# A sequence of four transformer layers' blocks on one core: the output projections' third share for ACT and POOL

## The chip, the cores and the metric

The kernel runs on one core of one Trainium2 chip. The metric is the device time of one execution in microseconds (us). The kernel before the change takes 793.25 us (median of 3 runs, 792.65 to 794.08).

The core has five engines with queues of their own: PE (TensorE, matrix products; PEld are its weight loads), DVE (VectorE), ACT (ScalarE), POOL (GpSimd) and SP (transfers). Each works through its own instructions in order; they meet through semaphores, which an instruction raises when it is done and on which a later one waits. Products land in PSUM, eight banks of 128 x 512 floats, which PE, DVE and ACT reach in this kernel; POOL works on SBUF alone.

## The reference

Two layers, each an attention and a feed-forward block with a residual and a layer normalisation behind each: attention with a position bias, a sparse Fourier product, dilated segment attention, and last a mixture of experts that is itself an attention. The change concerns only the end of the last block, for n = 2048 tokens (16 tiles of 128), 16 experts and 128 channels:

```
w = softmax(masked gates)                  # (n, 16), from the layer's input x
q, k, v = moe_proj(q_proj), moe_proj(k_proj), moe_proj(v_proj)
o = softmax(q k^T / sqrt(128)) v           # (n, 128)
out = einsum('ne,nh->enh', w, o) times o_proj, summed over e   # (n, 128)
x = layernorm(x + out)
```

So each tile of 128 tokens needs 16 products of its attention output with an expert's 128 x 128 matrix, each scaled per token by a gate weight w, and their sum, to which x is added before the normalisation.

## The kernel before

The kernel is one program with a written order for each engine; there is no planner. Up to about 718 us of the trace it computes the first three blocks and the last block's q, k, v and attention. Then come the output projections, the stage that the change rewrites.

The stage goes over 8 *pairs* of tiles; two pairs are a *quad* (4 tiles), and the final statistics are taken by quad. Variables: `a` is the pair's place in its quad, `u` the tile's place in its pair (0 or 1), `v` the quad's parity.

**PE.** Four experts side by side make a *group*, 128 x 512, one bank. Float products are split in two parts for accuracy, so a group is three matmuls (`product`, lines 1086 to 1088: high x high, high x low, low x high). The operand of a tile is its attention output in two parts: `op_hi` (a copy by ACT) and `op_lo` (the rest, a subtraction by POOL, `op_second`, line 591). A tile has four groups. The groups of experts 4 to 15 go to DVE (`group`, banks 0 to 3 in turn), the group of experts 0 to 3 goes to ACT (`first_group`, banks 4 to 7, two for each parity of pairs). In `out_quad` PE issues for each pair: DVE's groups of experts 4 to 7 of both tiles; the ACT groups of the *next* pair, which wait on `xc_set`, the op_lo of that pair; then DVE's other four groups.

**ACT.** `first_weighted` scales the four products of an ACT group by their weights, 128 columns at a time (line 1467), into `z_first` in SBUF, and raises `z0_sb` once a group. Then, once PE has done all DVE groups of the running pair, ACT copies the op_hi of the pair two further on; in each quad it also writes the normalised output of the quad before (`last_norm`, line 1490), which SP stores.

**POOL.** `first_sum` adds the four scaled parts of a tile: 256 columns onto 256 (line 657), 128 onto 128 (660), and the residual xb (662), into `y_acc`. In `sums_quad` POOL does, for each pair in order: the sums of tile 0 and tile 1 of the next pair; op_lo of both tiles of the pair after that (line 591); at the end of a quad the root of its variances (lines 678, 680).

**DVE.** Line 1891 multiplies each of the remaining products by its weight and adds it onto `y_acc`, 12 per tile, the two tiles in turn; the first of a tile waits for POOL's sum (`y0_set`). Each waits, through `acc_step`, until the last but one before it is done, which is the last one of the same tile. PE's bank waits go by the same `acc_step`. At a quad's end DVE takes the statistics (lines 1896 to 1906).

Of the kernel before, what the change touches and what calls it, by code (L numbers as in the profile page):

```python
# [23 lines left out]
ALU = mybir.AluOpType  # L24
ACT = mybir.ActivationFunctionType
# [34 lines left out]
E = 16  # L60
EPS = 1e-5
W3 = 3 * D
WC, NWC = 1024, 8
E_EARLY = NH // 2 * S // 4 // W3
LOADS_WE = 7
YR = 4


def build(nc, x, wq, wk, wv, wo, w_re, w_im, bias, w_qkv, w_out, sim, gates, p_q, p_k, p_v, p_o,
          ident, c_cos, c_sin, c_nsin, slopes, kpos, rank, rows, out):  # L70
    scale = float(DH) ** -0.5
# [5 lines left out]
    with ExitStack() as ctx:  # L77
# [44 lines left out]
        def bank(n, count=1):  # L122
            return psum[n // 4][:, n % 4 * QN:(n % 4 + count) * QN]
# [38 lines left out]
        w_cur = sb("w_cur", [P, QUAD, E])  # L162
        m_cur = sb("m_cur", [P, 2, 3])
        y_out = sb("y_out", [P, 2, QUAD, D])
        w_act = sb("w_act", [P, 2, 2, E])
        r_sum = sb("r_sum", [P, NT])
        kT_hi, kT_lo = sb("kT_hi", [P, NT * P], F32R), sb("kT_lo", [P, NT * P], F32R)
        f_p = probs[:].rearrange("p a b -> p (a b)")
# [70 lines left out]
        w_div, z0_ps, z0_sb, y0_set, w_act_set, y0_step = (  # L239
            sem(n) for n in ("w_div", "z0_ps", "z0_sb", "y0_set", "w_act_set", "y0_step"))  # L240
# [3 lines left out]
        v_set, acc_step, fin_step = sem("v_set"), sem("acc_step"), sem("fin_step")  # L244
        pool_step = sem("pool_step")
        q_hi_set, k_lo_set = sem("q_hi_set"), sem("k_lo_set")
        q_set, sc_ps, nmax_set, p_set, pt_ps, pt_sb, o_ps, o_sb = (
            sem(n) for n in ("q_set", "sc_ps", "nmax_set", "p_set", "pt_ps", "pt_sb", "o_ps", "o_sb"))
        fin_root = sem("fin_root")
        z_ps, w_set, fin_var, fin_std, fin_set = (  # L250
            sem(n) for n in ("z_ps", "w_set", "fin_var", "fin_std", "fin_set"))
# [222 lines left out]
        def _(pool):  # L474
# [165 lines left out]
            with pool.Fori(0, NT // 2 - 1) as i:  # L640
                for u in range(2):
                    t = 2 * i + u + 2
# [9 lines left out]
            def first_sum(pair, a, u, q, v):  # L652

                z, y = z_first[:, a, u], y_acc[:, v, 2 * a + u, :]
                n = 2 * pair + u
                pool.wait_ge(z0_sb, n + 5)
                pool.tensor_tensor(z[:, 0:2 * D], z[:, 0:2 * D], z[:, 2 * D:4 * D], ALU.add).then_inc(y0_step, 1)
                pool.wait_ge(y0_step, 2 * n + 1)
                pool.wait_ge(fin_set, q + 1)
                pool.tensor_tensor(y, z[:, 0:D], z[:, D:2 * D], ALU.add).then_inc(y0_step, 1)  # L660
                pool.wait_ge(y0_step, 2 * n + 2)
                pool.tensor_tensor(y, y, xb[:].rearrange("p t d -> p (t d)")[:, bass.ds(n * D, D)], ALU.add)\  # L662
                    .then_inc(y0_set, 1)

# [27 lines left out]
        def _(pe):  # L692
# [16 lines left out]
            for q in range(NQ):  # L709
# [4 lines left out]
                pair = bank(2 + 2 * (q % 2), 2)  # L714
# [169 lines left out]
            for n in range(-AHEAD, NU + 2):  # L884
# [8 lines left out]
                k = n - (NU - AHEAD)  # L893
# [189 lines left out]
            def product(dst, a, u, at, n):  # L1083

                hi, lo = op_hi[:, a, u, :], op_lo[:, a, u, :]
                pe.matmul(dst, hi, w_hi[:, at:at + n], start=True, stop=False)  # L1086
                pe.matmul(dst, hi, w_lo[:, at:at + n], start=False, stop=False)  # L1087
                return pe.matmul(dst, lo, w_hi[:, at:at + n], start=False, stop=True)  # L1088
# [70 lines left out]
            for b in range(NB):  # L1159
                with pe.Fori(b * KB // 2, (b + 1) * KB // 2 - b) as i:  # L1160
                    for u in range(2):
                        t = 2 * i + u
# [4 lines left out]

            def group(pair, a, n):  # L1170
                for u in range(2):

                    pe.wait_ge(acc_step, NT + 8 * (pair * 3 + n - 1))
                    product(bank((2 * (3 * a + n - 1) + u) % 4), a, u, E * W3 + n * 4 * D, 4 * D).then_inc(z_ps, 1)

            def first_group(pair, a):
                pe.wait_ge(xc_set, NT + QUAD + 2 * pair + 2)
                for u in range(2):
                    pe.wait_ge(z0_sb, 2 * pair + u + 1)
                    product(bank(4 + 2 * a + u), a, u, E * W3, 4 * D).then_inc(z0_ps, 1)  # L1180

            def out_quad(q, begin, end):
                for a in range(2):
                    pair = 2 * q + a
                    if not (begin and a == 0):
                        group(pair, a, 1)
                    if not (end and a == 1):
                        first_group(pair + 1, 1 - a)
                    group(pair, a, 2)
                    group(pair, a, 3)  # L1190


            pe.wait_ge(xc_set, NT + QUAD + 2)
            group(0, 0, 1)
            probs_T(NT - 1, 1)
            pe.wait_ge(pt_sb, 2 * NT + 2)
            first_group(0, 0)
            outputs(NT - 1, 1, NB - 1)
            pe.wait_ge(o_sb, NT + 2)
            out_quad(0, True, False)  # L1200
# [6 lines left out]
        def _(act):  # L1207
# [250 lines left out]

            def first_weighted(pair, a):

                act.wait_ge(z0_sb, 2 * pair + 4)
                weights_of(pair, a, NT // 2 + pair + 1)
                for u in range(2):
                    act.wait_ge(z0_ps, 2 * pair + u + 1)
                    act.wait_ge(y0_set, 2 * pair + u + 1)
                    for e in range(4):
                        ins = act.activation(z_first[:, a, u, e * D:(e + 1) * D],
                                             bank(4 + 2 * a + u)[:, e * D:(e + 1) * D], ACT.Copy,
                                             scale=w_act[:, a, u, e:e + 1])
                    ins.then_inc(z0_sb, 1)  # L1470

            def out_quad(q):
                for a in range(2):
                    pair = 2 * q + a
                    if pair + 1 == NT // 4:
                        act.wait_ge(w_div, 2)
                    if pair + 1 < NT // 2:
                        first_weighted(pair + 1, 1 - a)
                    if a == 0 and q:
                        last_norm(q - 1)  # L1480
                    act.wait_ge(z_ps, 6 * (pair + 1))
                    for u in range(2):
                        copy(op_hi[:, a, u, :], oT_all[:, bass.ds((2 * pair + 4 + u) % NT * P, P)])\
                            .then_inc(op_hi_set, 1)
# [19 lines left out]
        def _(dve):  # L1504
# [363 lines left out]
                dve.sem_inc(stored[u], 16)  # L1868


            per = QUAD * (E - 4)

            with dve.Fori(0, NQ // 2) as i:
                for v in range(2):
                    q = 2 * i + v
                    weights(q, NQ)
                    for a in range(2):
                        for n in range(1, E // 4):
                            for j in range(4):
                                for u in range(2):  # L1880
                                    t, e = 2 * a + u, 4 * n + j

                                    k = q * per + a * (per // 2) + 2 * (e - 4) + u
                                    z = bank((2 * (3 * a + n - 1) + u) % 4)[:, j * D:(j + 1) * D]
                                    if j == 0:
                                        dve.wait_ge(z_ps, q * 12 + a * 6 + 2 * (n - 1) + u + 1)
                                    if e == 4:
                                        dve.wait_ge(y0_set, q * QUAD + t + 5)
                                    else:
                                        dve.wait_ge(acc_step, NT + 8 + k - 1)  # L1890
                                    dve.scalar_tensor_tensor(out=y_acc[:, v, t, :], in0=z, scalar=w_cur[:, t, e:e + 1],  # L1891
                                                             in1=y_acc[:, v, t, :], op0=ALU.mult, op1=ALU.add)\
                                       .then_inc(acc_step, 1)
                    dve.wait_ge(acc_step, NT + 8 + (q + 1) * per)
                    for t in range(QUAD):
                        ins = dve.bn_stats(st[:, 0, t, :], y_acc[:, v, t, :])
                    ins.then_inc(fin_step, 1)
                    dve.wait_ge(fin_step, NT + 3 * q + 1)
                    dve.memset(tick[:, 0:1], 0.0).then_inc(fin_step, 1)
                    for t in range(QUAD):  # L1900
                        ins = dve.bn_aggr(mv[:, 0, t, :], st[:, 0, t, :])
                    ins.then_inc(fin_step, 1)
                    dve.wait_ge(fin_step, NT + 3 * q + 3)
                    dve.wait_ge(fin_std, q + 1)
                    dve.tensor_scalar(nb[:, 2 + v, :], mv[:, 0, :, 0], -1.0, None, ALU.mult).then_inc(fin_var, 1)
                    dve.tensor_scalar(ve[:, v, :], mv[:, 0, :, 1], EPS, None, ALU.add).then_inc(fin_var, 1)
# [48 lines left out]
```

## Time and profile before

| | |
|---|---|
| median of 3 runs | 793.25 us (792.65 to 794.08) |
| span of the profiled execution, first to last instruction | 791.8 us |
| its mean granted PE clock | 0.930 |
| busy: PE / DVE / ACT / POOL | 669.5 / 638.1 / 440.5 / 146.9 us |

The profile comes from one execution, whose time is given by its span; the runs' times hold what lies before and after it too. Busy time counts when an engine executes; idle time of an engine matters only where another waits for its result. [...] Matmuls overlap in PE's pipeline, so the distance between two starts, not the duration of one, says how fast they follow each other.

### The profile page before, as it was taken

What the parts mean: (1) busy time and instruction counts of PE and PEld (TensorE: products, weight loads), DVE (VectorE), ACT (ScalarE), POOL (GpSimd) and SP (SyncE); (2) the same over time, 40 slices, a digit from 0 to 9 for tenths busy, and PEclk for the clock granted to TensorE, in tenths of its full rate; (3) what the DMA queues carried; (4) which work ended last, traced back from release to release, by engine and by line L of the source; (5) the groups of instructions that cost most, each with busy time, mean ns of one, the idle gap of its engine ahead of it and who ended that gap; (6) DMA issues with size and microseconds to landing.
All of it is one profiled execution on the core that took longest, in us unless ns stands there. A gap on an engine that the chain in (4) does not pass through costs nothing.

```text
span 791.8 us, 16602 instructions
## 1 busy us (share of the span) xinstructions
PE 669.5 (85%) x5866; PEld 427.6 (54%) x5866; DVE 638.1 (81%) x1134; ACT 440.5 (56%) x961; POOL 146.9 (19%) x279
## 2 busy tenths in 40 slices
PE   7578888888888888899855886499999998998883
PEld 5223333333333333335634665499999997996652
DVE  2779999999999999965654667799999994554996
ACT  3059999999999999975442356111111114454442
POOL 6401000000000000001210117501111122123553
PEclk9569999999999999999975698599999999999998
DMA  7711111111111110006663000000000000000000
GB/s 201 223 25 33 33 32 33 31 33 31 33 32 32 32 31 3 2 3 137 134 171 95 4 5 1 0 1 1 0 1 0 0 0 1 0 0 1 14 14 26
DMA packets 28937, 28.72 MB, mean 36 GB/s; under 512 B 4952, under 2 KB 24920, under 8 KB 28152
## 3 DMA queue, kind: packets, MB, share of 16 engines
q1 hardware_dynamic: 27640, 26.99, 13.7%
q0 software_dynamic: 960, 0.79, 0.4%
q8 instruction: 41, 0.67, 0.4%
q14 instruction: 24, 0.20, 0.1%
q10 hardware_dynamic: 272, 0.07, 0.0%
HBM read 17.74 MB, written 4.98 MB: 29 GB/s over the span
## 4 chain that ended last, share of the span: by engine, by line
PE 52%; ACT 19%; issue 11%; DVE 10%; SPq 3%; DMA 2%; POOL 2%; ACTq 0%; DVEq 0%; POOLq 0%
ACT probs L1254 16%; PE ps_hi L775 13%; PE ps_lo L1086 7%; PE ps_lo L1088 7%; PE ps_lo L1087 7%; PE ps_hi L789 4%; PE ps_hi L1146 2%; DVE probs L1891 2%; PE ps_hi L1137 1%; DVE mx L1644 1%; PE ps_lo L975 1%; ACT mrow L1209 1%; PE ps_hi L819 1%; SPq L340 1%; PE ps_lo L1128 1%
## 5 line engine op out<-in xcount | busy, mean ns | idle before, releaser
L1561 DVE TENSOR_REDUCE mx<-ps_lo 128x2 f32<-128x1024 f32 x256 | 306.3, 1224 | 8.6 <-PE ps_lo L752 5.3
L1254 ACT ACTIVATE probs<-ps_hi 128x512 f32<-128x512 f32 x512 | 277.9, 597 | 44.0 <-PE ps_hi L775 31.0
L789 PE MATMUL ps_hi<-probs,v_blk 128*32 128x256 f32 x2048 | 164.7, 393 | 6.0 <-ACT mrow L1209 5.8
L775 PE MATMUL ps_hi<-q,k 28*128 28x512 f32 x512 | 129.7, 500 | 31.5 <-ACT probs L1254 14.6
L752 PE MATMUL ps_lo<-k,q 26*128 26x512 f32 x512 | 132.9, 516 | 4.6 <-DVE mx L1561 4.2
L1825 DVE SCALAR_TENSOR_TENSOR tok_cur<-ps_lo,w_cur,tok_cur 128x384 f32<-128x384 f32 x240 | 127.8, 609 | 6.1 <-PE ps_lo L1088 4.8
L775 PEld LDWEIGHTS ps_hi<-q,k 28*128 28x128 f32 x512 | 48.7, 183 | 141.5 <-ACT probs L1254 116.2
L1086 PE MATMUL ps_lo<-w_hi,op_hi 128*128 128x384 f32 (+1 forms) x304 | 108.1, 356 | 20.0 <-DVEq L1786 10.1
L1087 PE MATMUL ps_lo<-w_lo,op_hi 128*128 128x384 f32 (+1 forms) x304 | 105.5, 347 | 0.0
L1088 PE MATMUL ps_lo<-w_hi,op_lo 128*128 128x384 f32 (+1 forms) x304 | 105.5, 347 | 0.0
L789 PEld LDWEIGHTS ps_hi<-probs,v_blk 128*32 128x32 f32 x2048 | 42.0, 108 | 71.0 <-ACT probs L1254 59.2
L1209 ACT ACTIVATE op_hi<-xT 128x128 fp32r<-128x128 f32 (+1 forms) x40 | 10.0, 301 | 118.0 <-PE ps_lo L1088 118.0
L1086 PEld LDWEIGHTS ps_lo<-w_hi,op_hi 128*128 128x128 f32 x304 | 57.9, 191 | 28.2 <-DVE probs L1891 16.3
L555 POOL TENSOR_SCALAR mx_parts<-mx_all 128x8 fp32r<-128x8 f32 x32 | 7.4, 232 | 300.5 <-DVE mx_all L1555 293.6
L1088 PEld LDWEIGHTS ps_lo<-w_hi,op_lo 128*128 128x128 f32 x304 | 57.9, 191 | 2.1
L1087 PEld LDWEIGHTS ps_lo<-w_lo,op_hi 128*128 128x128 f32 x304 | 58.0, 191 | 1.3
L752 PEld LDWEIGHTS ps_lo<-k,q 26*128 26x128 f32 x512 | 49.4, 189 | 11.0 <-DVE mx L1561 9.4
L1891 DVE SCALAR_TENSOR_TENSOR probs<-ps_lo,w_cur,probs 128x128 f32<-128x128 f32 x192 | 50.5, 341 | 5.4 <-POOL probs L662 4.4
L591 POOL TENSOR_TENSOR op_lo<-xT,op_hi 128x128 fp32r<-128x128 f32 x40 | 17.9, 472 | 114.4 <-ACT op_hi L1209 114.4
L1146 PEld LDWEIGHTS ps_hi<-probs,v_tok 128*128 128x128 f32 x256 | 31.2, 193 | 2.4 <-DVE probs L1842 1.0
L1317 ACT ACTIVATE probs<-ps_lo 128x1024 f32<-128x1024 f32 x12 | 12.3, 1023 | 35.8 <-PE ps_lo L959 35.8
L1146 PE MATMUL ps_hi<-probs,v_tok 128*128 128x128 f32 x256 | 31.4, 276 | 0.8 <-DVE probs L1842 0.8
(256 smaller groups left out, 819.2 us busy)
## 6 DMA issues: line engine op xcount, KB each, us to landing
q<-q_parts SPq DMA_DIRECT2D x30, 192.0 KB
k<-k_parts SPq DMA_DIRECT2D x32, 96.0 KB
q_rep<-qk_p SPq DMA_DIRECT2D x24, 128.0 KB, 2.4
q_parts<-qk_hi SPq DMA_DIRECT2D x8, 256.0 KB, 4.8
k_rep<-qk_p SPq DMA_DIRECT2D x24, 64.0 KB, 2.1
xa<-in_L_attn_x SPq DMA_DIRECT2D x4, 256.0 KB, 3.3
q_parts<-qk_lo SPq DMA_DIRECT2D x4, 256.0 KB, 5.2
q<-mrow SPq DMA_DIRECT2D x64, 4.0 KB
```

Source lines behind the costliest of these rows:

```text
L752: mm = pe.matmul(bank(2 * (m % 2) + a), q0[rows, h * QN + i * P:h * QN + (i + 1) * P], k0[rows, k_at:k_at + QN], start=True, stop=True)
L775: mm = pe.matmul(bank(4 + (2 * n + a) % 3), k0[rows, k_at:k_at + P], q0[rows, h * QN:(h + 1) * QN], start=True, stop=True)
L789: mm = pe.matmul(o_bank()[32 * r:32 * r + 32, 0:OW], v_all[:, at:at + 32], probs0[:, n % P_RING, r * OW:(r + 1) * OW], start=(kb == 0), st ...
L1086: pe.matmul(dst, hi, w_hi[:, at:at + n], start=True, stop=False)
L1087: pe.matmul(dst, hi, w_lo[:, at:at + n], start=False, stop=False)
L1088: return pe.matmul(dst, lo, w_hi[:, at:at + n], start=False, stop=True)
L1146: mm = pe.matmul(bank(6 + u)[:, 0:P], v_tok[:, (b * KB + kb) * D:(b * KB + kb + 1) * D], pT_cur[:, u, kb * P:(kb + 1) * P], start=(kb == 0 ...
L1209: return act.activation(dst, src, ACT.Copy)
L1254: act.activation(probs0[:, n % P_RING, a * QN:(a + 1) * QN], bank(4 + (2 * n + a) % 3), ACT.Exp).then_inc(s0_free, 1)
L1561: dve.reduce_max(mx2[:, j % 2, :, i, kh], bank(2 * (m % 2), 2).rearrange("p (a n) -> p a n", a=2), AX_X).then_inc(max0_done, 1)
L1825: dve.scalar_tensor_tensor(out=tok_cur[:, a, u, :], in0=y, scalar=w, in1=tok_cur[:, a, u, :], op0=ALU.mult, op1=ALU.add).then_inc(y_free, 1)
L1891: dve.scalar_tensor_tensor(out=y_acc[:, v, t, :], in0=z, scalar=w_cur[:, t, e:e + 1], in1=y_acc[:, v, t, :], op0=ALU.mult, op1=ALU.add)\
```

## The change

For the second tile of each pair (u = 1) the group of experts 4 to 7 moves from DVE to ACT and POOL as well. Per pair ACT then scales three groups instead of two (`Z_FIRST`: tile 0's and tile 1's first group, and tile 1's second), POOL adds tile 1's second group onto its first, 512 columns wide, before it goes on as before, and DVE has 20 multiply-adds instead of 24, 12 for tile 0 and 8 for tile 1, in the order 0, 1, 0, 1, 0 four times (`Z_TURNS`). An instruction of DVE that follows one of the same tile waits for that one. DVE's five groups of a pair (`Z_LAST`) have the banks 0, 1, 2, 3, 7, ACT's three have 4, 5, 6, each one bank for every pair; a group waits until the same bank has been read in the pair before (`Z_READ`, the last reader's number). PE's order in a pair becomes: DVE's groups 0 and 1, the next pair's ACT groups 0 and 1, DVE's groups 2 and 3, the next pair's ACT group 2, DVE's group 4. `sums_quad` keeps its order.

```diff
+Z_FIRST = ((0, 0), (1, 0), (1, 1))
+Z_LAST = ((0, 1), (1, 2), (0, 2), (1, 3), (0, 3))
+N_FIRST, N_LAST = len(Z_FIRST), len(Z_LAST)
+Z_BANKS = (0, 1, 2, 3, 7)
+Z_TURNS = (0, 1, 0, 1, 0) * 4
+PER = len(Z_TURNS)
...
+Z_READ = [max(n for n, place in enumerate(Z_PLACES) if place[2] == d) for d in range(N_LAST)]
...
-                pool.wait_ge(z0_sb, n + 5)
+                pool.wait_ge(z0_sb, N_FIRST * pair + (5, 7)[u])
+                if u == 1:
+                    pool.tensor_tensor(z[:], z[:], z_first[:, a, 2], ALU.add).then_inc(y0_step, 1)
+                    pool.wait_ge(y0_step, 5 * pair + 3)
                 pool.tensor_tensor(z[:, 0:2 * D], z[:, 0:2 * D], z[:, 2 * D:4 * D], ALU.add).then_inc(y0_step, 1)
...
+            def group(pair, a, d):
+                u, n = Z_LAST[d]
+                pe.wait_ge(acc_step, NT + 8 + PER * pair - PER + Z_READ[d] + 1)
+                product(bank(Z_BANKS[d]), a, u, E * W3 + n * 4 * D, 4 * D).then_inc(z_ps, 1)
+
+            def first_group(pair, a, j):
+                u, n = Z_FIRST[j]
                 pe.wait_ge(xc_set, NT + QUAD + 2 * pair + 2)
+                pe.wait_ge(z0_sb, N_FIRST * pair + j + 2)
+                product(bank(4 + j), a, u, E * W3 + n * 4 * D, 4 * D).then_inc(z0_ps, 1)
...
                     if not (begin and a == 0):
+                        group(pair, a, 0)
                         group(pair, a, 1)
                     if not (end and a == 1):
-                        first_group(pair + 1, 1 - a)
+                        first_group(pair + 1, 1 - a, 0)
+                        first_group(pair + 1, 1 - a, 1)
                     group(pair, a, 2)
                     group(pair, a, 3)
+                    if not (end and a == 1):
+                        first_group(pair + 1, 1 - a, 2)
+                    group(pair, a, 4)
...
+            pe.wait_ge(o_sb, NT + 1)
+            for j in range(N_FIRST):
+                first_group(0, 0, j)
...
+                for j, (u, n) in enumerate(Z_FIRST):
+                    act.wait_ge(z0_ps, N_FIRST * pair + j + 1)
                     act.wait_ge(y0_set, 2 * pair + u + 1)
                     for e in range(4):
+                        ins = act.activation(z_first[:, a, j, e * D:(e + 1) * D],
+                                             bank(4 + j)[:, e * D:(e + 1) * D], ACT.Copy,
+                                             scale=w_act[:, a, u, 4 * n + e:4 * n + e + 1])
                     ins.then_inc(z0_sb, 1)
...
+                        for n, (u, e, d) in enumerate(Z_PLACES):
+                            t, k = 2 * a + u, (2 * q + a) * PER + n
+                            z = bank(Z_BANKS[d])[:, e % 4 * D:(e % 4 + 1) * D]
+                            if e % 4 == 0:
+                                dve.wait_ge(z_ps, (2 * q + a) * N_LAST + d + 1)
+                            if n < 2:
+                                dve.wait_ge(y0_set, q * QUAD + t + 5)
+                            else:
+                                dve.wait_ge(acc_step, NT + 8 + k - (Z_TURNS[n - 1] != u))
```

## Rows read from the trace of the kernel before

**Rows 1.** The page's busy tenths in 40 slices of 19.8 us: DVE and granted clock.
```profile
DVE  2779999999999999965654667799999994554996
...
PEclk9569999999999999999975698599999999999998
```

**Rows 2.** Windows: length; busy PE, PEld, DVE, ACT, POOL; clock; DMA, GB/s.
```profile
727.00:785.00 58.00, 44.82 (x175) 30.99 (x173) 55.68 (x231) 24.52 (x89) 33.67 (x66) 1.00 0.05 14
```

**Rows 3.** Lines of DVE from 725 to 785, by form: count, busy us, mean ns.
```profile
L1891 DVE SCALAR_TENSOR_TENSOR probs<-ps_lo,w_cur,probs 128x128 f32<-128x128 f32 x192 | 50.5, 341 | 5.4 <-POOL probs L662 4.4 <-DVE w_cur L1806 0.7 <-PE ps_lo L1088 0.2
```

**Rows 4.** Timeline of DVE in the stage: start, length, instructions merged.
```profile
727.62 12.50 DVE L1891 SCALAR_TENSOR_TENSOR probs<-ps_lo,w_cur,probs 128x128 f32<-128x128 f32 x47 [1.43 <-POOL probs L662]
740.15 0.87 DVE L1896 BATCH_NORM_STATS2 st<-probs 128x6 f32<-128x128 f32 x4
...
771.84 12.49 DVE L1891 SCALAR_TENSOR_TENSOR probs<-ps_lo,w_cur,probs 128x128 f32<-128x128 f32 x48 [0.22 <-DVE w_cur L1806]
```

**Rows 5.** Waits from 727 to 785: total us, times, longest.
```profile
PEld ps_lo L1086 <- DVE probs L1891: 16.3, 16, 2.3
```

**Rows 6.** Timeline of all engines, from one pair's ACT groups to the next's.
```profile
747.81 0.39 PE L1086 MATMUL ps_hi<-w_hi,op_hi 128*128 128x512 f32 x1
...
748.75 2.17 ACT L1467 ACTIVATE probs<-ps_hi,w_act 128x128 f32<-128x128 f32 x8 [2.16 <-issue]
...
749.20 0.39 PE L1086 MATMUL ps_lo<-w_hi,op_hi 128*128 128x512 f32 x1
...
749.97 0.74 POOL L657 TENSOR_TENSOR probs<-probs 128x256 f32<-128x256 f32 x1 [2.51 <-ACT probs L1467]
...
751.74 0.73 POOL L657 TENSOR_TENSOR probs<-probs 128x256 f32<-128x256 f32 x1
...
753.50 0.89 POOL L591 TENSOR_TENSOR op_lo<-xT,op_hi 128x128 fp32r<-128x128 f32 x2
...
754.52 0.49 PE L1086 MATMUL ps_hi<-w_hi,op_hi 128*128 128x512 f32 x1
```

**Rows 7.** Lines of POOL by form, whole span: count, busy us, mean ns.
```profile
L546 POOL TENSOR_TENSOR w_lo<-big,w_hi 128x1024 fp32r<-128x1024 f32 x8 | 19.1, 2420 | 19.7 <-ACT w_hi L1209 19.7
...
L657 POOL TENSOR_TENSOR probs<-probs 128x256 f32<-128x256 f32 x16 | 11.7, 733 | 24.6 <-ACT probs L1467 24.6
...
L678 POOL TENSOR_TENSOR rstd<-ve,half 128x4 f32<-128x4 f32 x4 | 4.1, 1018 | 9.1 <-DVE ve L1906 9.1
```

**Rows 8.** Timeline of all engines where the stage starts.
```profile
721.75 0.51 PE L1086 MATMUL ps_hi<-w_hi,op_hi 128*128 128x512 f32 x1 [0.78 <-DVE probs L1842]
...
722.79 2.17 ACT L1467 ACTIVATE probs<-ps_hi,w_act 128x128 f32<-128x128 f32 x8 [1.08 <-issue]
...
725.21 0.28 ACT L1209 ACTIVATE xT<-ps_hi 128x128 f32<-128x128 f32 x1 [0.24 <-PE ps_hi L1146]
...
725.54 0.50 PE L1086 MATMUL ps_hi<-w_hi,op_hi 128*128 128x512 f32 x1 [0.37 <-ACT xT L1209]
```

**Rows 9.** Timeline of PE: what follows an idle (its length in brackets).
```profile
397.72 0.50 PE L937 MATMUL ps_lo<-k_rep,q_rep 64*128 64x64 bf16 x6 [2.38 <-DVE mx L1644]
...
655.74 1.09 PE L1137 MATMUL ps_hi<-ident_sb,probs 128*128 128x128 f32 x8 [1.96 <-ACT probs L1209]
...
658.00 0.63 PE L1129 MATMUL ps_lo<-kT_lo,q_hi 128*128 x1
658.43 0.63 PE L1130 MATMUL ps_lo<-kT_hi,q_lo 128*128 x1
...
759.37 0.50 PE L1086 MATMUL ps_lo<-w_hi,op_hi 128*128 128x512 f32 x1 [1.85 <-DVE probs L1891]
```

**Rows 10.** Windows around two clock levels, columns as in rows 2.
```profile
397.60:400.60 3.00, 1.88 (x13) 1.48 (x13) 0.89 (x4) 2.84 (x9) 0.55 (x1) 0.50 0.46 114
...
657.00:660.00 3.00, 2.58 (x6) 2.11 (x7) 0.56 (x1) 0.47 (x1) 0.89 (x3) 0.50 0.00 0
660.50:663.50 3.00, 3.00 (x27) 2.91 (x26) 1.72 (x4) 0.59 (x2) 0.74 (x2) 1.00 0.02 5
```

More of the change, by code:

```diff
@@ L66, with z_places @@
 YR = 4
+Z_FIRST = ((0, 0), (1, 0), (1, 1))
[4 more added lines that the diff above has]
+PER = len(Z_TURNS)
+def z_places():
+    places, first, seen = [], [8 - 4 * (u == 0) for u in range(2)], [0, 0]
+    for u in Z_TURNS:
+        e = first[u] + seen[u]
+        seen[u] += 1
+        places.append((u, e, Z_LAST.index((u, e // 4))))
+    return places
+Z_PLACES = z_places()
+Z_READ = [max(n for n, place in enumerate(Z_PLACES) if place[2] == d) for d in range(N_LAST)]
 def build(nc, x, wq, wk, wv, wo, w_re, w_im, bias, w_qkv, w_out, sim, gates, p_q, p_k, p_v, p_o,
@@ L173, in build @@
         oT_all = xT
-        z_first = f_p[:, 0:2048].rearrange("p (a u n) -> p a u n", a=2, u=2)
-        y_acc = f_p[:, 2048:3072].rearrange("p (v t n) -> p v t n", v=2, t=QUAD)
+        z_first = f_p[:, 0:2 * N_FIRST * 4 * D].rearrange("p (a g n) -> p a g n", a=2, g=N_FIRST)
+        y_acc = f_p[:, 3072:4096].rearrange("p (v t n) -> p v t n", v=2, t=QUAD)
         ld_dft = sem("ld_dft")
@@ L655, in first_sum @@
                 n = 2 * pair + u
-                pool.wait_ge(z0_sb, n + 5)
+                pool.wait_ge(z0_sb, N_FIRST * pair + (5, 7)[u])
+                if u == 1:
+                    pool.tensor_tensor(z[:], z[:], z_first[:, a, 2], ALU.add).then_inc(y0_step, 1)
+                    pool.wait_ge(y0_step, 5 * pair + 3)
                 pool.tensor_tensor(z[:, 0:2 * D], z[:, 0:2 * D], z[:, 2 * D:4 * D], ALU.add).then_inc(y0_step, 1)
-                pool.wait_ge(y0_step, 2 * n + 1)
+                pool.wait_ge(y0_step, 5 * pair + (1, 4)[u])
                 pool.wait_ge(fin_set, q + 1)
                 pool.tensor_tensor(y, z[:, 0:D], z[:, D:2 * D], ALU.add).then_inc(y0_step, 1)
-                pool.wait_ge(y0_step, 2 * n + 2)
+                pool.wait_ge(y0_step, 5 * pair + (2, 5)[u])
                 pool.tensor_tensor(y, y, xb[:].rearrange("p t d -> p (t d)")[:, bass.ds(n * D, D)], ALU.add)\
@@ L1166, in _ @@
             outputs(NT - 2, 0, NB - 1)
[L1170 to L1176, printed above, removed]
+            def group(pair, a, d):
[4 more added lines that the diff above has]
+                u, n = Z_FIRST[j]
                 pe.wait_ge(xc_set, NT + QUAD + 2 * pair + 2)
-                for u in range(2):
-                    pe.wait_ge(z0_sb, 2 * pair + u + 1)
-                    product(bank(4 + 2 * a + u), a, u, E * W3, 4 * D).then_inc(z0_ps, 1)
+                pe.wait_ge(z0_sb, N_FIRST * pair + j + 2)
+                product(bank(4 + j), a, u, E * W3 + n * 4 * D, 4 * D).then_inc(z0_ps, 1)
             def out_quad(q, begin, end):
@@ L1185, in out_quad @@
                     if not (begin and a == 0):
+                        group(pair, a, 0)
                         group(pair, a, 1)
                     if not (end and a == 1):
-                        first_group(pair + 1, 1 - a)
+                        first_group(pair + 1, 1 - a, 0)
+                        first_group(pair + 1, 1 - a, 1)
                     group(pair, a, 2)
                     group(pair, a, 3)
+                    if not (end and a == 1):
+                        first_group(pair + 1, 1 - a, 2)
+                    group(pair, a, 4)
             pe.wait_ge(xc_set, NT + QUAD + 2)
+            group(0, 0, 0)
             group(0, 0, 1)
@@ L1196, in _ @@
             pe.wait_ge(pt_sb, 2 * NT + 2)
-            first_group(0, 0)
+            pe.wait_ge(o_sb, NT + 1)
+            for j in range(N_FIRST):
+                first_group(0, 0, j)
             outputs(NT - 1, 1, NB - 1)
@@ L1459, in first_weighted @@
             def first_weighted(pair, a):
-                act.wait_ge(z0_sb, 2 * pair + 4)
+                act.wait_ge(z0_sb, N_FIRST * pair + 1)
                 weights_of(pair, a, NT // 2 + pair + 1)
-                for u in range(2):
-                    act.wait_ge(z0_ps, 2 * pair + u + 1)
+                for j, (u, n) in enumerate(Z_FIRST):
+                    act.wait_ge(z0_ps, N_FIRST * pair + j + 1)
                     act.wait_ge(y0_set, 2 * pair + u + 1)
                     for e in range(4):
-                        ins = act.activation(z_first[:, a, u, e * D:(e + 1) * D],
-                                             bank(4 + 2 * a + u)[:, e * D:(e + 1) * D], ACT.Copy,
-                                             scale=w_act[:, a, u, e:e + 1])
+                        ins = act.activation(z_first[:, a, j, e * D:(e + 1) * D],
+                                             bank(4 + j)[:, e * D:(e + 1) * D], ACT.Copy,
+                                             scale=w_act[:, a, u, 4 * n + e:4 * n + e + 1])
                     ins.then_inc(z0_sb, 1)
@@ L1480, in out_quad @@
                         last_norm(q - 1)
-                    act.wait_ge(z_ps, 6 * (pair + 1))
+                    act.wait_ge(z_ps, N_LAST * (pair + 1))
                     for u in range(2):
@@ L1868, in _ @@
                 dve.sem_inc(stored[u], 16)
-            per = QUAD * (E - 4)
             with dve.Fori(0, NQ // 2) as i:
@@ L1877, in _ @@
                     for a in range(2):
[L1878 to L1894, printed above, removed]
+                        for n, (u, e, d) in enumerate(Z_PLACES):
[7 more added lines that the diff above has]
+                                dve.wait_ge(acc_step, NT + 8 + k - (Z_TURNS[n - 1] != u))
+                            dve.scalar_tensor_tensor(out=y_acc[:, v, t, :], in0=z, scalar=w_cur[:, t, e:e + 1],
+                                                     in1=y_acc[:, v, t, :], op0=ALU.mult, op1=ALU.add)\
+                               .then_inc(acc_step, 1)
+                    dve.wait_ge(acc_step, NT + 8 + (q + 1) * 2 * PER)
                     for t in range(QUAD):
```

## Prediction

> **What bounds the kernel now.** I read the page's slices first: the last three, from 732 us, are the output projections, which the change rewrites, and the DVE row shows 9, 9 and 6 there, the 6 holding the end [rows 1]. [...] By shapes nearly all of it is the multiply-adds of line 1891, 192 of them, 50.5 us, so 0.263 us from one start to the next though one lasts 0.341 [rows 3]. DVE's timeline shows them back to back in long runs, 47 in 12.50 us and 48 in 12.49 [rows 4]. Waits agree: the loads of PE's weights wait 16.3 us for DVE to free a bank [rows 5]. A pair of tiles costs DVE 24 x 0.263 = 6.3 us and half a quad's statistics, near 1 us: 7.3 us, and eight pairs fill the stage.
>
> Then I looked for what runs close behind. There is a loop from pair to pair through three engines, read from one stretch of the timeline [rows 6]. PE starts the two ACT groups of a pair at 747.81; ACT starts on the first at 748.75; POOL starts its sums at 749.97, needs 1.77 us for a tile (749.97 to 751.74) and 1.76 for the next, and only then, its queue being in order, makes the op_lo of the pair after (753.50, 0.89 us); PE starts that pair's ACT groups at 754.52. Round trip 6.71 us. It hides behind DVE's 7.3 by 0.6 us.
>
> **The change, part by part.** *DVE.* Eight pairs x 4 multiply-adds fewer: 32 x 0.263 = 8.4 us. The new order, tiles 0 1 0 1 0 repeated, puts tile 0 behind itself at three places inside a pair, and there the instruction waits for the one just before. The statistics behind the last multiply-add start 0.03 us after its end (740.12 to 740.15 [rows 4]), so such a step takes 0.34 + 0.03 = 0.37 instead of 0.26: 0.11 us, 24 times, 2.6 us. A lower bound is 0, the upper 0.3 each. DVE's own pair: 20 x 0.263 + 0.33 + 0.95 = 6.5 us. If nothing else were late, the stage would lose 5.8 us.
>
> *The loop.* The third ACT group (tile 1, experts 4 to 7) is only the fifth product that PE issues after op_lo: two ACT groups, two DVE groups, then it. POOL's sum of tile 1 waits for it, and op_lo of the next pair still stands behind that sum. The loop from op_lo to op_lo is now:
> - PE: two products took 1.39 us (747.81 to 749.20), so four take 2.78; from the fifth's start to ACT's start as now 0.94; and 0.10 more, since the first matmul after a wait lasts 0.49 instead of 0.39 (754.52 against 747.81) [rows 6]. 3.82.
> - ACT: four scalings and the hand-over to POOL, 748.75 to 749.97: 1.22.
> - POOL: the new 512-wide addition. The trace has none; 256 wide takes 0.733, 1024 wide 2.420 [rows 7]. On the line between them 512 takes 0.733 + (2.420 - 0.733)/3 = 1.30, which I take; the ends are those two rows. With 0.07 to the next instruction 1.37.
> - POOL: tile 1's sum as now, 1.77; op_lo 0.89 and 0.13 until PE starts: 1.02.
>
> Sum 9.20 us, against DVE's 6.5. DVE is no longer the bound; POOL's queue behind the third group is. Tile 0's sum costs the loop nothing: it fits between ACT's first and third group. So does the root at a quad's end, 1.02 us [rows 7]. Behind ACT's third scaling stand the final normalisation and the op_hi copies; they run beside POOL's 3.1 us of adding. PE's bank waits cost nothing: a DVE group waits until the same bank was read in the pair before, and DVE, which itself waits for tile 1's sum, is through by then; an ACT group, now with one bank instead of two, waits for a scaling that op_lo comes after anyway. At the start PE also waits for the last but one output's copy, done 2 us earlier. If DVE's lateness did reach a PE wait it would only lengthen the loop.
>
> [...]
>
> *The start.* The first three ACT groups instead of two, from 721.75, push the attention's last outputs 0.7 us back; ACT scales from 722.79, 2.17 us for two groups, so 3.3 for three, and its copy of the last output, at 725.21 today, comes near 726.1. PE starts pair 1's ACT groups at 726.4 instead of 725.54 [rows 8]. POOL, two of whose sums have the extra addition now, has summed pair 0 at 729.3 and pair 1 at 734.4; op_lo of pair 2 follows and its ACT groups start at 735.4.
>
> *The end.* Five more loops: pair 7's groups start at 735.4 + 5 x 9.2 = 781.4. Then 3.82 + 1.22 + 1.37 + 1.77 = 8.2: at 789.6 DVE takes up tile 1 of pair 7, with 19 multiply-adds left, 18 x 0.263 + 3 x 0.11 + 0.35 = 5.4, to 795.0. Today the last one ends at 771.84 + 12.49 = 784.33 [rows 4]. What follows (statistics, root, normalisation, store) is unchanged. **+10.7 us** with PE at the clock it has now.
>
> *The clock.* In the loop PE now has eight products, 5.6 us, and then nothing to do for 9.2 - 5.6 = 3.6 us, six times. Today its longest idle in the stage is 1.85 us, and the clock stays [rows 9]. [...] At 0.50 a 128x512 matmul comes 0.43 us after the one before (658.00, 658.43 [rows 9]) instead of 0.23 (1.39 for six [rows 6]), a product of three 1.29 instead of 0.69. [...] Bounds per loop: 0, and 5 x 0.60 = 3.0. A low stretch like the second, between 3 and 3.5 us at half speed, costs half its length if PE is busy in it, 1.6 us; I take this, six times: **+9.6 us**.
>
> Sum: span 791.8 + 10.7 + 9.6 = 812.1. The median of the runs, 793.25, lies 1.45 above the span, outside the first and last instruction, and that stays: 813.5.
>
> **The rivals.**
> 1. *The loop holds, the clock does too:* +10.7, so 804.0. For it: in this stage the clock never left 1.00, with 44.82 of 58 us of PE busy [rows 2]; the short bursts may be enough. [...]
> [...]
> 3. *Faster: DVE remains the bound.* Place: op_lo. Were it, or tile 1's sum, not in the way of PE, the stage would go at DVE's 6.5 us a pair, -5.8, so 787.5. It decides at 7.3 us a loop: below, the kernel is faster, above, slower. For it: POOL is busy for 33.67 of 58 us only [rows 2], and the loop hides today. Against it: it hides by 0.6, and four further products (2.8 us) and an addition of 1.37 enter it, while only tile 0's sum, 1.76, leaves it. Even with the addition at its lower end, 0.73, and no wait of PE, 8.6 remain.
> 4. *No change,* the loop near 7.3: 1.9 us of each round, the addition and more, would have to be hidden by something that I do not see; the time would stay at 793.3.
>
> **How the numbers follow.** Forecast 0.58 (813.5); rival 1 0.26 (804); rival 2 0.06 (822); rival 3 0.07 (787.5); rival 4 0.03 (793.3). The addition's ends change seven additions on the path by 7 x -0.57 = -4.0 and 7 x 1.12 = +7.8; the waits between neighbours on DVE at most 0.6, as only the last pair's count. The forecast's own range, with the clock costing 0.7 to 2.4 us a loop, is 806 to 819. Rival 1 with the addition at its lower end gives 800; part of rival 2 lies above 819. I give 800 to 820, which leaves out rivals 3 and 4, most of rival 2 and the edges of the rest, 2 in 10. About 0.2% is what a measurement of this kernel can tell from no change: faster 0.07, the same 0.03, slower 0.90.
>
> **What would show it.** Right: PE's ACT groups of one pair and the next 9 to 11 us apart; DVE waiting 2 us and more in each pair for POOL's last addition (the addition of xb), no longer PE for DVE; POOL's 512-wide addition near 1.3 us; multiply-adds 160 in number; granted clock 0.50 in stretches after idles of PE over 3 us. Wrong: PE's ACT groups less than 7.3 us apart, or op_lo ready before PE has done its DVE groups; a clock of 1.00 throughout would leave 804.

## The result: 814.6 us, 2.5% slower

The changed kernel takes 814.61 us (median of 4 runs, 813.5 to 817.22); the kernel before, beside it, 793.66 (4 runs, 792.65 to 795.42). The ratio is 1.0246, its 95% interval 1.0202 to 1.029. The profiled execution took 814.29 us with a span of 812.5, where the prediction had 812.1.

The slices of the page, DVE and granted clock (the share of its full speed that PE was given), answer to [rows 1]; a slice is 20.3 us now, and the stage fills the last four. There DVE reads 7, 6, 6, 5, where it had 9, 9, 6, and the clock 7, 8, 8, 7, where it had 9, 9, 8.

```profile
DVE  1789999999999999945545767899999965537665
PEclk9679999999999999999865996799999999997887
```

The stage from its first ACT group to its last multiply-add, as one window: length, then busy time (instructions) of PE, PEld, DVE, ACT and POOL, granted clock, DMA share, GB/s. First before, then after.

```profile
721.75:784.33 62.58, 49.70 (x202) 35.21 (x202) 55.73 (x230) 27.61 (x100) 36.42 (x70) 1.00 0.04 13
```

```profile
722.00:805.00 83.00, 57.36 (x202) 43.77 (x202) 51.65 (x198) 35.98 (x132) 46.81 (x78) 0.85 0.03 10
```

The stage is 20.4 us longer; the predicted sum was 20.3. DVE has 32 instructions fewer, as the change says, and ACT and POOL 32 and 8 more, but no engine is full any more, as DVE was before with 55.68 of 58.00 us [rows 2]: PE, the busiest now, works 57 of 83 us, at 0.85 of its full clock. Where nobody is full and everybody is late, a loop of waits is the first suspect. Two rows of the waits in this stage (total us, times, longest) name it:

```profile
PE ps_hi L1108 <- POOL op_lo L610: 19.3, 6, 3.4
DVE probs L1914 <- PE ps_lo L1110: 15.7, 6, 3.2
```

PE waits for POOL's op_lo, where its weight loads waited for DVE before [rows 5], and DVE waits for PE, whose products come behind the same wait. One turn of the loop in the timeline (start, length, instruction, in brackets the idle time before it and who ended it) answers to [rows 6]:

```profile
767.64 0.86 POOL L610 TENSOR_TENSOR op_lo<-xT,op_hi 128x128 fp32r<-128x128 f32 x2
...
768.63 0.49 PE L1108 MATMUL ps_hi<-w_hi,op_hi 128*128 128x512 f32 x1 [3.32 <-POOL op_lo L610]
...
769.83 2.37 ACT L1496 ACTIVATE probs<-ps_hi,w_act 128x128 f32<-128x128 f32 x8 [4.88 <-issue]
...
772.42 2.03 DVE L1914 SCALAR_TENSOR_TENSOR probs<-ps_lo,w_cur,probs 128x128 f32<-128x128 f32 x7 [2.00 <-PE ps_lo L1110]
...
773.96 1.14 ACT L1496 ACTIVATE probs<-ps_hi,w_act 128x128 f32<-128x128 f32 x4 [1.76 <-PE ps_hi L1110]
...
775.18 1.28 POOL L677 TENSOR_TENSOR probs<-probs 128x512 f32<-128x512 f32 x1 [2.33 <-ACT probs L1496]
...
778.29 0.87 POOL L610 TENSOR_TENSOR op_lo<-xT,op_hi 128x128 fp32r<-128x128 f32 x2
...
778.37 1.77 DVE L1914 SCALAR_TENSOR_TENSOR probs<-ps_lo,w_cur,probs 128x128 f32<-128x128 f32 x6 [1.61 <-POOL probs L684]
...
779.29 0.60 PE L1108 MATMUL ps_hi<-w_hi,op_hi 128*128 128x512 f32 x1 [3.33 <-POOL op_lo L610]
```

Read it downward: op_lo frees PE at 768.63; the third ACT group comes fifth, so ACT reaches it only at 773.96; POOL, which has waited 2.33 us, adds it at 775.18, then sums tile 1, and only then makes op_lo for the next pair, which PE gets at 779.29. That is 10.66 us a turn. The same turn cut by the granted clock:

```profile
769.50:772.60 3.10, 3.10 (x9) 2.38 (x8) 1.06 (x5) 2.29 (x8) 1.60 (x4) 0.50 0.00 0
773.00:776.00 3.00, 2.96 (x14) 2.10 (x12) 2.66 (x11) 2.04 (x7) 0.82 (x1) 1.00 0.00 0
776.00:779.20 3.20, 0.00 (x0) 0.00 (x0) 1.58 (x7) 1.14 (x5) 2.92 (x6) 1.00 0.27 82
```

PE has nothing to do from 776.00 on, as POOL works. In each of the six turns that begin behind such an idle the clock falls to 0.50, from 0.6 us before to 1.1 us after the first matmul of the burst (here 0.65 us after it, behind the idle of 3.32; 769.50 to 772.60 stands at 0.50), and is back at 1.00 before the burst ends. The chain of waits shows the last turn matmul by matmul (start, length):

```profile
789.00 0.86 POOL op_lo L610 x2
789.90 0.79 PE ps_hi L1108
790.69 0.43 PE ps_hi L1109
791.12 0.43 PE ps_hi L1110
...
792.83 0.43 PE ps_lo L1108
...
794.44 0.23 PE ps_hi L1108
...
795.44 0.89 ACT probs L1496 x3
796.39 1.29 POOL probs L677
...
799.80 0.09 issue
799.89 0.17 DVE probs L1914
```

Matmuls come 0.43 us apart until 793.25 and 0.23 after it: the low stretch lies on the five products that the loop waits for, here on the first three of them.

### The profile page after: what moved, and what is told of

The parts are those of the page before. It is cut to its first block and busy times, and to the rows that moved or that the text cites. A ratio compares the mean times of both kernels' runs of the same rounds, so it can differ in the third digit from the quotient of the medians.

```text
span 812.5 us, 16583 instructions
## 1 busy us (share of the span) xinstructions
PE 675.9 (83%) x5866; PEld 433.9 (53%) x5866; DVE 633.9 (78%) x1102; ACT 449.8 (55%) x993; POOL 157.6 (19%) x287
## 5 line engine op out<-in xcount | busy, mean ns | idle before, releaser
L1108 PE MATMUL ps_lo<-w_hi,op_hi 128*128 128x384 f32 (+1 forms) x288 | 102.0, 354 | 10.5 <-DVEq L1815 10.1
L1109 PE MATMUL ps_lo<-w_lo,op_hi 128*128 128x384 f32 (+1 forms) x288 | 100.2, 348 | 0.0
L1110 PE MATMUL ps_lo<-w_hi,op_lo 128*128 128x384 f32 (+1 forms) x288 | 100.0, 347 | 0.0
L1108 PEld LDWEIGHTS ps_lo<-w_hi,op_hi 128*128 128x128 f32 x288 | 56.0, 194 | 13.4 <-issue 10.1
L1914 DVE SCALAR_TENSOR_TENSOR probs<-ps_lo,w_cur,probs 128x128 f32<-128x128 f32 x128 | 37.6, 344 | 27.9 <-PE ps_lo L1110 15.7
L1109 PEld LDWEIGHTS ps_lo<-w_lo,op_hi 128*128 128x128 f32 x288 | 56.0, 194 | 1.6
L1110 PEld LDWEIGHTS ps_lo<-w_hi,op_lo 128*128 128x128 f32 x288 | 55.5, 193 | 1.8
L1496 ACT ACTIVATE probs<-ps_hi,w_act 128x128 f32<-128x128 f32 x96 | 27.0, 374 | 40.8 <-issue 29.0
L1108 PE MATMUL ps_hi<-w_hi,op_hi 128*128 128x512 f32 x32 | 15.9, 495 | 20.4 <-POOL op_lo L610 19.3
```

Of the source, the lines that this page charges most:

```text
L1496: ins = act.activation(z_first[:, a, j, e * D:(e + 1) * D], bank(4 + j)[:, e * D:(e + 1) * D], ACT.Copy, scale=w_act[:, a, u, 4 * n + e:4 ...
```

## The experiments

My theory had two parts: the new loop (PE's third group, ACT, POOL's addition, tile 1's sum, op_lo) is longer than DVE's share of a pair, about +10 us; and the idle that it leaves PE brings the low clock in nearly every turn, about +10 more. Rivals were other parts of the change that could cost by themselves: the bank layout of five and three, and DVE's neighbours of one tile. Each kernel is the changed kernel with the edit shown (the last one, experiment 6 with it). The stretch ahead of the stage, which no edit touches, starts the stage anywhere from 719.5 to 728.6 us in these profiled runs, so stages are compared as well as times.

**1. The third ACT group right behind the first two, on PE.** POOL's order is as changed, so op_lo still stands behind tile 1's sum, but the group is no longer fifth.

```
-  first_group(pair + 1, 1 - a, 0)
-  first_group(pair + 1, 1 - a, 1)
+  for j in range(N_FIRST):
+      first_group(pair + 1, 1 - a, j)
   group(pair, a, 2)
   group(pair, a, 3)
-  first_group(pair + 1, 1 - a, 2)
   group(pair, a, 4)
```

> The changed kernel with one thing moved: PE issues the next pair's third ACT group directly behind the first two, ahead of DVE's groups 2 and 3. Theory (the loop through the third group, ACT, POOL's sum of tile 1 and op_lo sets the stage): the third group is the third product after op_lo instead of the fifth, but ACT, which scales three groups in 3.21 us, is then in line: 0.94 + 0.10 until ACT starts, 3.21 + 0.12, the addition with its gap 1.36, the sum 1.77, op_lo and PE's start 1.0: 8.5 us a loop instead of 9.2 at full clock, PE's idle about 2.9 us instead of 3.4. Six to seven loops: 4 to 5 us less, near 810 (808 to 811), the clock still falling in most loops. Rival A (the bank layout, one bank for each of ACT's and DVE's groups, is what holds PE up): PE's order then changes nothing or makes it worse, 814 to 818. Rival B (DVE's order with neighbours of one tile): nothing, 814.6.

Measured: 803.62 us, ratio to before 1.0101 (1.0068 to 1.0135). The window of the stage, and ACT's scalings of two turns:

```profile
719.54:790.67 71.13, 53.47 (x202) 40.57 (x202) 49.80 (x198) 35.85 (x132) 46.90 (x78) 0.90 0.04 12
...
760.46 3.65 ACT L1494 ACTIVATE probs<-ps_hi,w_act 128x128 f32<-128x128 f32 x12 [4.45 <-issue]
...
769.37 3.20 ACT L1494 ACTIVATE probs<-ps_hi,w_act 128x128 f32<-128x128 f32 x12 [3.21 <-issue]
```

The place of the third group is worth 83.0 - 71.1 = 11.9 us of the stage. I had expected 4 to 5 us, a miss in size. The loop was sized well: between PE's first ACT groups of two pairs lie 8.43 and 8.36 us where the clock stays (8.5 expected). But I let the low clock cost as much as before. With the three groups in a row the loop goes through ACT's twelve scalings, 1.07 us a group, and PE at a clock of 0.50 needs 1.29 for one (three matmuls 0.43 apart), so a turn at the low clock is later by less: the scalings take 3.65 instead of 3.20 us, and the three turns with a low stretch take 8.80, 8.94 and 9.33 us, 0.4 to 1.0 more, where the changed kernel's lose 1.4 and more. The low clock itself became rarer too, 13.65 us in the stage instead of 25.5.

**2. op_lo ahead of tile 1's sum, on POOL.** PE's order is as changed.

```
-  for u in range(2):
-      first_sum(pair + 1, 1 - a, u, q + a, (v + a) % 2)
+  first_sum(pair + 1, 1 - a, 0, q + a, (v + a) % 2)
   for u in range(2):
       ...
       op_second((t + QUAD) % NT, a, u)
+  first_sum(pair + 1, 1 - a, 1, q + a, (v + a) % 2)
```

> The changed kernel with one thing moved: in POOL's queue op_lo of the pair after the next stands between the sums of tile 0 and tile 1 instead of behind both. Theory: the addition and the sum of tile 1, 3.1 us, leave the loop; it goes by PE's sixth product, ACT's third scaling and op_hi, op_lo: about 6.5 us, and 8.1 where ACT's final normalisation (1.65) stands ahead of op_hi, which is every second pair; 7.3 on average, as before the change. PE's idles shrink below 2.6 us, so the clock mostly stays at 1.00. Time 791 to 797. Rival A (bank layout) and rival B (DVE's neighbours): 814, unchanged. Rival C (POOL's whole load, 6.4 us of work a pair, is the bound, not its order): hardly less, 812 to 815.

Measured: 795.1 us, ratio 0.9985 (0.9954 to 1.0016), no difference from before. The window of the stage and PE's timeline:

```profile
723.67:786.40 62.73, 49.89 (x202) 36.30 (x202) 49.90 (x198) 35.62 (x132) 46.76 (x78) 0.96 0.05 14
...
746.50 0.50 PE L1109 MATMUL ps_lo<-w_hi,op_hi 128*128 128x512 f32 x1 [1.62 <-DVE probs L1915]
...
748.68 0.49 PE L1109 MATMUL ps_hi<-w_hi,op_hi 128*128 128x512 f32 x1 [0.45 <-POOL op_lo L610]
```

With op_lo out of tile 1's way the whole 20 us are gone: 62.73 against 62.58. PE waits for DVE again, 1.62 us here, and for op_lo only twice, 0.45 and 0.34. The low clock is down to 4.64 us of the stage though nothing was done about the clock: it went with PE's idle. (An idle of 2.05 us at 761.31 brought it, so the 2.6 us of the expectation was no safe mark.) The bank layout and DVE's neighbours are still here, so neither costs what was lost. Nothing is gained on the kernel before, though DVE has less to do: it waits 9.9 us in six times for POOL's sums, where it waited 4.4 in two.

**3. PE without the idle, the loop left as it is.** The second DVE group's product is made five times into the same bank (the last is the one that is read), so that PE works while POOL adds.

```
 def group(pair, a, d, again=0):
     ...
+    for _ in range(again):
+        product(bank(Z_BANKS[d]), a, u, E * W3 + n * 4 * D, 4 * D)
     product(...).then_inc(z_ps, 1)
...
-    group(pair, a, 1)
+    group(pair, a, 1, again=4)
```

> The changed kernel, and PE computes DVE's group 1 of each pair but the first five times over instead of once (the same product into the same bank; only the last one reports), 2.8 us of work put into the 3.4 us in which PE idles. Theory: the loop stays at 9.1 us, as PE has nothing to do there; the granted clock stays at 1.00 in the stage, and the time falls by what the clock cost, 1.6 to 1.8 us in each of six loops: 803 to 806, though PE does 84 matmuls more. If the low clock costs nothing (the loop then being longer for another reason): 814 or more. If the further products come in the way of DVE's group 1: up to 0.5 us a loop more than that, 807.

Measured: 804.29 us, ratio 1.0117 (1.0055 to 1.0179). The window of the stage and PE's ACT groups of two pairs:

```profile
720.01:792.98 72.97, 65.67 (x286) 51.85 (x286) 51.84 (x198) 35.40 (x132) 47.10 (x78) 1.00 0.04 11
...
760.87 0.49 PE L1108 MATMUL ps_hi<-w_hi,op_hi 128*128 128x512 f32 x1 [0.65 <-POOL op_lo L610]
...
769.97 0.49 PE L1108 MATMUL ps_hi<-w_hi,op_hi 128*128 128x512 f32 x1 [0.65 <-POOL op_lo L610]
```

84 matmuls that do nothing for the result make the stage 10.0 us shorter than the changed kernel's. The clock stays at 1.00 and a turn takes 9.10 us (predicted 9.20). So the loss splits: the loop costs 72.97 - 62.58 = 10.4, the clock 83.0 - 72.97 = 10.0. The split is good to some 0.4 us, for at the very end DVE now waits that long for the further products (POOL's last sum ends at 787.17, DVE goes on at 787.60).

**4. Half the filler.** The same with again=2.

> The changed kernel, and PE computes DVE's group 1 three times over instead of once: 1.4 us of work in the 3.4 us of idle, so that some 2.0 us remain in each loop. With the five-fold version the clock stayed at 1.00. Theory: an idle of 2.0 us among so much work brings fewer falls or none: at most 10 us of the stage at 0.50 (25.5 without the further products), the stage 73 to 77 us. If the falls come from the idle's place and not its length: 20 us or more at 0.50 and a stage of 80 or more.

Measured, one run: 816.84 us (its stage starts at 728.63). The window, and PE's ACT groups of three pairs, and two windows behind them:

```profile
728.63:807.55 78.92, 62.66 (x244) 48.50 (x244) 51.66 (x198) 35.75 (x132) 46.99 (x78) 0.91 0.04 11
...
761.96 0.50 PE L1108 MATMUL ps_hi<-w_hi,op_hi 128*128 128x512 f32 x1 [2.00 <-POOL op_lo L610]
772.64 0.49 PE L1108 MATMUL ps_hi<-w_hi,op_hi 128*128 128x512 f32 x1 [1.97 <-POOL op_lo L610]
781.73 0.49 PE L1108 MATMUL ps_hi<-w_hi,op_hi 128*128 128x512 f32 x1 [2.00 <-POOL op_lo L610]
...
762.10:765.10 3.00, 3.00 (x8) 2.37 (x9) 0.67 (x3) 1.61 (x6) 0.48 (x1) 0.53 0.00 0
772.80:775.80 3.00, 3.00 (x14) 2.46 (x15) 2.29 (x9) 2.12 (x8) 1.71 (x4) 1.00 0.00 0
```

A miss: I thought that half the filler would do more. Behind the idle of 2.00 us at 761.96 the clock was down (0.53 in the window from 762.10) and the turn took 10.68 us; behind the one of 1.97 at 772.64 it was at 1.00, and the turn took 9.09, the length of experiment 3. In all it was low for 14.5 us of the stage, and the idle's length alone does not say in which turn: idles of 2.02, 2.00, 2.00 and 1.92 us brought it, that of 1.97 did not.

**5. The addition made small.** again=2, and POOL adds 16 of the 512 columns; the rest of experts 4 to 7 of every second tile is left out of the sum.

```
-  pool.tensor_tensor(z[:], z[:], z_first[:, a, 2], ALU.add)
+  pool.tensor_tensor(z[:, 0:16], z[:, 0:16], z_first[:, a, 2, 0:16], ALU.add)
```

> The changed kernel, with two things: POOL adds only the first 16 of the third group's 512 columns (the rest of experts 4 to 7 of every second tile is left out of the result), and PE computes DVE's group 1 three times over instead of once, to keep its clock up. The loop of 9.1 us, with the clock at 1.00, loses what the addition costs above a small one, 1.29 - 0.2 = 1.1 us, seven times. Theory: the stage, from the first ACT group to DVE's last multiply-add, takes 72.97 us with PE kept busy and the whole addition; it takes 65 to 66 here, and ACT groups of neighbouring pairs stand 8.0 us apart. If the addition is hidden (rival: POOL's order matters, its length not): 73, and 9.1 us apart.

Measured: 796.49 us, ratio 1.0001 (0.9963 to 1.0039). The window, PE's ACT groups, and POOL's line by form (busy us, mean ns):

```profile
722.25:787.37 65.12, 55.84 (x244) 44.11 (x244) 50.78 (x198) 35.37 (x132) 38.65 (x78) 1.00 0.04 13
...
750.75 0.49 PE L1108 MATMUL ps_hi<-w_hi,op_hi 128*128 128x512 f32 x1 [0.94 <-POOL op_lo L610]
758.76 0.49 PE L1108 MATMUL ps_hi<-w_hi,op_hi 128*128 128x512 f32 x1 [0.93 <-POOL op_lo L610]
...
L677 POOL TENSOR_TENSOR probs<-probs 128x16 f32<-128x16 f32 x8 | 1.8, 222 | 6.4 <-ACT probs L1498 6.4
```

A turn takes 8.01 us, 1.09 less than the 9.10 of experiment 3, and the addition is 1.29 - 0.22 = 1.07 shorter: all of it stands on the loop. Even nearly free of it, the loop is longer than DVE's 7.3 us a pair before the change, from which on the change would have gained, so a faster addition alone does not save it.

**6. Both moves, and op_hi ahead of the normalisation.** Experiments 1 and 2 together; besides, ACT makes op_hi, which op_lo needs, before it normalises the quad that is done.

```
   # ACT, out_quad
-  if a == 0 and q:
-      last_norm(q - 1)
   act.wait_ge(z_ps, N_LAST * (pair + 1))
   for u in range(2):
       copy(op_hi...)
+  if a == 0 and q:
+      last_norm(q - 1)
```

> Both moves, and ACT copies op_hi before the final normalisation instead of after it. Theory: the loop is about 6.1 us in every pair (ACT's third scaling ends 4.4 after PE's start, op_hi 0.5, op_lo 0.9, hand-overs 0.3), under DVE's 6.5 a pair; DVE is the bound again and the stage gains what its 32 multiply-adds fewer give: 787 to 790, faster than before the change. POOL's 6.4 us a pair is close behind; if POOL is the bound instead, 789 to 792. Rivals A and B: 805 or more, since the layout and DVE's order are those of the change.

Measured: 797.39 us, ratio 1.0025 (0.999 to 1.006). The window, then DVE's and POOL's timeline:

```profile
728.60:790.01 61.41, 49.59 (x202) 36.52 (x202) 49.88 (x198) 35.73 (x132) 46.83 (x78) 0.97 0.05 14
...
756.09 3.71 DVE L1913 SCALAR_TENSOR_TENSOR probs<-ps_lo,w_cur,probs 128x128 f32<-128x128 f32 x13 [0.93 <-POOL probs L684]
...
763.16 1.02 POOL L701 TENSOR_TENSOR rstd<-ve,half 128x4 f32<-128x4 f32 x1 [1.28 <-DVE ve L1928]
```

A miss: I expected 787 to 790 us, and the stage is only 1.2 us shorter than before. DVE now waits for POOL's sums (0.93 us at 756.09), and POOL, whose queue is in order, waits 1.28 us at the quad's root for DVE's statistics, with the next sums behind it: each stands in the other's way.

**7. The root later too.** Experiment 6, and POOL takes the root of a quad behind op_lo of the next quad's first pair; POOL's loop over the quads is written out for this.

```
+  if a == 0 and q:
+      root_of(q - 1, 1 - v)
   first_sum(pair + 1, 1 - a, 1, q + a, (v + a) % 2)
```

> The version with both moves and op_hi first, and one thing more: POOL takes the root of a quad's variances behind op_lo of the next quad's first pair, instead of ahead of that quad's sums, where it waited about 1 us for DVE's statistics and kept the sums 1.3 us longer. Theory: in that version POOL's queue, full from pair 1 on, makes DVE wait 0.5 to 0.9 us in each second pair; without the root in the way DVE is the bound alone. The stage takes 59 to 60 us instead of 61.4 there and 62.6 before the change: 2.5 to 3.5 us faster than before, a ratio of 0.996. If POOL's whole load is the bound, 61 us, and a ratio of 0.998 to 1.0.

Measured: 794.88 us over 12 runs, ratio 0.996 (0.9926 to 0.9994) to the kernel before beside it (797.92). It is the one version here whose interval lies below 1, and only just: the kernel before moved by more between sets of runs (medians of 793.66, 795.04 and 797.92), so the gain rests on the stage of one profiled execution. The window, POOL's timeline at a root, and DVE's:

```profile
725.46:785.74 60.28, 49.33 (x202) 36.48 (x202) 49.89 (x198) 35.73 (x132) 46.81 (x78) 0.97 0.05 14
...
733.03 3.71 DVE L1914 SCALAR_TENSOR_TENSOR probs<-ps_lo,w_cur,probs 128x128 f32<-128x128 f32 x13 [3.12 <-POOL probs L684]
...
746.68 0.87 POOL L610 TENSOR_TENSOR op_lo<-xT,op_hi 128x128 fp32r<-128x128 f32 x2
747.51 1.01 POOL L704 TENSOR_TENSOR rstd<-ve,half 128x4 f32<-128x4 f32 x1
748.75 1.29 POOL L677 TENSOR_TENSOR probs<-probs 128x512 f32<-128x512 f32 x1
...
767.15 3.19 DVE L1914 SCALAR_TENSOR_TENSOR probs<-ps_lo,w_cur,probs 128x128 f32<-128x128 f32 x11 [0.81 <-POOL probs L684]
```

The root no longer waits. The stage is 2.3 us shorter than before. The relief itself is real: DVE has 55.73 - 49.89 = 5.84 us less to do. But it is idle for 60.28 - 49.89 = 10.4 us instead of 6.85, so 3.5 of the 5.84 turned into waits. For POOL's sums it waits 7.1 us in four times (0.81 at 767.15), where [rows 3] has 4.4. Of these 2.7 us more, 1.7 come once, at the stage's start: DVE's first run on both tiles waits 3.12 us at 733.03, where the kernel before has 1.43 [rows 4], since tile 1 of pair 0 now has the third group and its addition ahead of its sum. What would bring back the rest was not tried.

## Why the prediction held, and where it did not

*The loop.* Right in kind and size: 9.20 us a turn predicted, 9.10 measured where the clock is held; +10.7 predicted for the stage, +10.4 measured. Experiments 1 and 2 show that the order makes it: the one shortens the loop, the other breaks it, and they take back 11.9 and 20.3 us with the same work in the stage.

*The addition.* The line between the 256- and 1024-wide rows [rows 7] gave 1.30 us; it measures 1.286. In proportion to the 1024-wide row alone it would have been 1.21; the 0.222 us that 16 columns take (experiment 5) shows a part of the time, about 0.19 us, that does not shrink with the width.

```profile
L677 POOL TENSOR_TENSOR probs<-probs 128x512 f32<-128x512 f32 x8 | 10.3, 1286 | 13.6 <-ACT probs L1496 13.6
```

*The clock.* The weakest step beforehand was my estimate of 1.6 us a loop, from one low stretch (657 to 660 at 0.50, 1.00 again from 660.5 [rows 10]) and from the idles of 1.96 and 2.38 us about which the clock stood at 0.50 [rows 9, rows 10], both shorter than the 3.6 us to come. It came out: 9.6 predicted, 10.0 measured. The idles are 2.64, 3.35, 3.34, 3.32, 3.33 and 3.28 us (3.6 predicted), and each brought a fall. That the sum fits so well is in part luck: the prediction had six falls alike. Five of them last 3.4 us, and cost 1.4 to 1.6 us where two neighbouring turns show it (a turn less 9.10), and one, from 745.4, lasts 6.8 us and costs 2.8. The rest of the 25.5 us, 1.6 us, lies behind PE's last product. Rival 1, the same loop with a full clock, was put at 804.0; experiment 3 is that kernel, and takes 804.29. Rival 2 (822) had the clock at 0.50 through the whole stage; it was there for 25.5 of 83.0 us.

*The steps of the ACT groups.* Predicted 10.8 us apart (9.2 + 1.6), measured 9.00, 10.53, 11.94, 10.66, 10.66 and 10.61; the five from 735.50 to 789.90 make 10.88 on average, and 735.50 itself was put at 735.4.

*DVE's waits: half wrong.* I wrote that DVE would wait for POOL's last addition and "no longer PE for DVE". The second holds but for 0.9 us; the first does not, as a bound of each pair: three pairs have it, 1.6 us each, and 3.0 and 3.1 us lie at the stage's start. In the lines of DVE, by form (count, busy us, mean ns, idle before and by whom):

```profile
L1914 DVE SCALAR_TENSOR_TENSOR probs<-ps_lo,w_cur,probs 128x128 f32<-128x128 f32 x128 | 37.6, 344 | 27.9 <-PE ps_lo L1110 15.7 <-POOL probs L684 11.0 <-DVE w_cur L1835 0.7
L1914 DVE SCALAR_TENSOR_TENSOR probs<-ps_hi,w_cur,probs 128x128 f32<-128x128 f32 x32 | 11.1, 346 | 2.3 <-PE ps_hi L1110 1.9
```

DVE waits longer for PE (15.7 us) than for POOL's sums (11.0). Three of the five DVE groups of a pair come behind the next pair's ACT groups in PE's queue and so behind its op_lo; the prediction had DVE through with a pair by then. It did not show in the time, as the loop took what was predicted without it.

*DVE's own share.* 160 multiply-adds (128 and 32 in these rows), as the count said. Their price was right too: 8.4 - 2.6 = 5.8 us less, and 5.84 in experiment 7.

*Rival 3, DVE as the bound.* Rightly given little, but its price was wrong. I put the stage at 5.8 us less once op_lo was out of the way; experiments 2, 6 and 7 take it out of the way and get nothing, 1.2 and 2.3 us. The step that failed there is that DVE would then be full: POOL with 46.8 us of work in 60 and an order to keep is late with its sums, for which DVE waits 9.9, 8.4 and 7.1 us in these three, 1.7 of the surplus over 4.4 at the stage's start alone.

## What to carry to other kernels

Before moving work from a full engine to an idle one, follow the loop that comes back to its start, in order of each queue: here 5.8 us less on the bound put four products and an addition into a loop with 0.6 us to spare, and took only one sum out of it. Then look at what the new idle does to TensorE's clock; here that was half of the loss, 10.0 of 20.4 us. And when such a move fails, change the order before giving it up: here one sum moved behind op_lo took back all 20 us.

## What the hardware showed that I had not expected

- Nearly the same idle brought the low clock in one turn and not in another: in experiment 4 those of 1.92, 2.00, 2.00 and 2.02 us did (14.5 us of the stage at a clock of 0.50 in all), that of 1.97 did not. Idles of 0.59 to 0.94 in experiments 3 and 5 did not either (at most 0.2 us of the stage, at its end).
- The low clock has no fixed price: 0.42 us for each us of it in the changed kernel, where the loop waits for PE's products (10.0 / 23.9, without the 1.6 us behind PE's last product), 0.44 in experiment 4 ((78.92 - 72.97) / 13.6, without the 0.9 us at its end), and 0.4 to 1.0 us for a stretch of 3.4, some 0.1 to 0.3, where the loop goes through ACT's scalings (experiment 1).
- Redundant matmuls can pay where PE would idle: 84 of them took 10.0 us off the stage.
- POOL's additions and subtractions lie within 0.03 us of one line from 16 to 1024 columns: 0.222, 0.733, 1.286 and 2.420 us for 16, 256, 512 and 1024 (the last is a subtraction [rows 7]), about 0.19 us and 2.2 ns a column.
